# A test-time-training layer with a gated feed-forward on one core: weight pieces issued from another queue, reads of the first tile's scan put first, the last tile's output by batch

## The reference, cut to what matters

```
k = rope(x @ Wk.T);  v = x @ Wv.T                # x: (2, 4096, 512), 16 heads of 32
for each block of 16 tokens (a scan):             # state W: 32x32 per batch and head, from eye
    z = k_block @ W
    W = W - k_block.T @ ((z - v_block) * 2 / (16 * 32))
out = layernorm(z of all blocks, gamma, beta) @ Wo.T
x1  = layernorm(x + out)
y   = (silu(x1 @ gate.T * gate_s) * (x1 @ up.T * up_s)) @ down.T * down_s     # 1408 hidden
result = layernorm(x1 + y)
```

## Time and profile before

| | |
|---|---|
| median of 3 runs | 1947.25 us |
| lowest, highest | 1944.1, 1949.56 us |
| profiled execution, its own time | 1950.08 us |
| its span, first to last instruction | 1948.3 us |
| mean granted TensorE clock | 0.981 |
| PE busy | 1855.2 us (95%) |
| DVE, POOL, ACT busy | 1178.1 (60%), 640.9 (33%), 547.9 us (28%) |
| chain that ended last | PE 73%, DVE 14%, DMA 4%, SP's queue 4% |

### The profile page before, as it was taken

One profiled execution on the slowest core, in us unless ns is written; L12 is line 12 of the kernel. 1 busy time (PEld: TensorE's weight loads), 2 busy tenths in 40 slices (PEclk: granted clock), 3 DMA queues, 4 the chain that ended last, 5 costly groups with the idle time before them and its releaser, 6 DMA issues.

```text
span 1948.3 us, 60606 instructions
## 1 busy us (share of the span) xinstructions
PE 1855.2 (95%) x25792; PEld 1478.8 (76%) x25792; DVE 1178.1 (60%) x2608; ACT 547.9 (28%) x1236; POOL 640.9 (33%) x776
## 2 busy tenths in 40 slices
PE   7569999999999999999999999999999999999897
PEld 4347777777777777777777787777778777777776
DVE  3456666656666666666666566566666666666543
ACT  2122223232322223222222232222322222232222
POOL 2113333333333333333333333333333333333333
PEclk9689999999999999999999999999999999999899
DMA  8665454455455445545445554544554544455210
GB/s 265 214 211 154 135 154 141 139 149 164 148 153 154 125 139 166 166 141 158 138 136 146 163 156 143 153 134 131 167 164 141 155 147 133 145 152 156 84 57 23
DMA packets 302497, 287.26 MB, mean 147 GB/s; under 512 B 42769, under 2 KB 252305, under 8 KB 302097
## 3 DMA queue, kind: packets, MB, share of 16 engines
q1 hardware_dynamic: 295952, 265.26, 45.8%
q10 hardware_dynamic: 6272, 18.09, 2.8%
HBM read 152.65 MB, written 139.20 MB: 150 GB/s over the span
## 4 chain that ended last, share of the span: by engine, by line
PE 73%; DVE 14%; DMA 4%; SPq 4%; ACT 2%; issue 2%; ACTq 0%; POOL 0%; DVEq 0%; POOLq 0%
PE gu_acc L778 31%; PE work L759 21%; PE down_acc L790 12%; PE scan_acc L731 4%; DVE x_tok L945 3%; PE scan_acc L748 3%; DVE state L1016 3%; DVE hid L1021 2%; DVE stats L931 2%; SPq L306 2%; DMA z_scr<-v_rows 2%; ACT hid L562 1%; DVE turned L950 1%; DMA landed<-x1T_scr 1%; SPq L350 1%
## 5 line engine op out<-in xcount | busy, mean ns | idle before, releaser
L496 POOL TENSOR_TENSOR hid_lo<-hid,hid_hi 128x256 fp32r<-128x256 f32 x352 | 263.5, 748 | 646.0 <-ACT hid_hi L572 638.2
L778 PE MATMUL gu_acc<-x_hi,gw 128*128 128x256 f32 x1372 | 376.0, 307 | 8.2 <-DVE hid L1021 2.3
L562 ACT ACTIVATE hid<-gu_acc,gate_scale 128x256 f32<-128x256 f32 x343 | 162.6, 474 | 786.0 <-PE gu_acc L778 786.0
L1021 DVE SCALAR_TENSOR_TENSOR hid<-gu_acc,up_scale,hid 128x256 f32<-128x256 f32 x343 | 165.6, 483 | 319.9 <-ACT hid L562 319.7
L778 PE MATMUL gu_acc<-x_lo,gw 128*128 128x256 f32 x1372 | 340.3, 281 | 0.0
L778 PE MATMUL gu_acc<-x_hi,uw 128*128 128x256 f32 x1372 | 339.7, 280 | 0.0
L778 PE MATMUL gu_acc<-x_lo,uw 128*128 128x256 f32 x1372 | 339.1, 280 | 0.0
L1016 DVE SCALAR_TENSOR_TENSOR state<-scan_acc,half_step,state 128x256 f32<-128x256 f32 x512 | 223.4, 478 | 173.5 <-PE scan_acc L748 168.8
L778 PEld LDWEIGHTS gu_acc<-x_hi,gw 128*128 128x128 f32 x1372 | 258.5, 188 | 44.4 <-DVE hid L1021 18.1
L790 PE MATMUL down_acc<-dw,hid_hi 128*128 128x512 f32 x704 | 282.3, 401 | 2.3 <-POOL hid_lo L496 2.2
L790 PE MATMUL down_acc<-dw,hid_lo 128*128 128x512 f32 x704 | 279.1, 397 | 0.0
(11 more groups left out here) (114 smaller groups left out, 2223.7 us busy)
## 6 DMA issues: line engine op xcount, KB each, us to landing
x_fm<-xT SPq DMA_DIRECT2D x64, 256.0 KB, 3.5
k_scr<-k_tok SPq DMA_DIRECT2D x32, 512.0 KB, 6.7
k_rows<-k_scr SPq DMA_DIRECT2D x512, 32.0 KB, 2.0
z_scr<-v_rows SPq DMA_DIRECT2D x32, 512.0 KB, 3.2
z_tok<-z_scr SPq DMA_DIRECT2D x512, 32.0 KB, 1.8
x_tok<-x SPq DMA_DIRECT2D x32, 512.0 KB, 5.8
out<-x_tok SPq DMA_DIRECT2D x32, 512.0 KB, 3.4
v_rows<-v_scr SPq DMA_DIRECT2D x488, 32.0 KB, 2.0
```

The source lines that it names most:

```text
L496: pool.tensor_tensor(hid_lo[m % RING][:], hid[m % 2][:], hid_hi[m % RING][:].bitcast(F32), ALU.subtract).then_inc(hid_lo_ready, 1)
L562: act.activation(hid[m % 2][:], gu_bank(n, m)[:, 0:TOK], ACT.Silu, scale=gate_scale[:, m:m + 1]).then_inc(silu_done, 1)
L778: mm = pe.matmul(gu_bank(n, m)[:, k * TOK:(k + 1) * TOK], lhsT=w[:, c, m * P:(m + 1) * P].bitcast(dt), rhs=part[:, c].bitcast(dt), start=( ...
L1021: dve.scalar_tensor_tensor(hid[m % 2][:], gu_bank(n, m)[:, TOK:2 * TOK], up_scale[:, m:m + 1], hid[m % 2][:], ALU.mult, ALU.mult).then_inc ...
```

## The change

Four things change.

1. All 24 DMAs of the feed-forward's weights move from ACT's program to POOL's, and to other slots: the four gate copies to tick -1 (ahead of any other wait on POOL), two up copies to tick 0, the rest to tick 1, the last two loads to slot 0 of tick 2. `WEIGHED` puts all twelve looks into tick 2.
2. SP's order in tick 1: z of tile 0 is stored and read first; the store of v(1, 1) comes after the first half of the z reads, and the k rows of tile 1 after all of them. Its v rows are now issued there, by SP, and no longer by ACT.
3. In every tick DVE does the end of tile t-4 (`normalize(2, yn, ...)`) in slot 1, behind `step_state` and the first norm of tile t-2, and not in slot 0.
4. The last tile's output is done by batch and on DVE (`finish_last`), with a pow for each batch on POOL and two stores.

```diff
-WEIGHED = {(1, 13): (0,), (1, 15): (1,), (2, 1): (2,), (2, 3): (3,), (2, 6): (4,), (2, 8): (5,), (2, 10): (6,), (2, 11): (7,),
-           (2, 12): (8,), (2, 13): (9, 10, 11)}
+WEIGHED = {(2, 1): (0,), (2, 2): (1,), (2, 3): (2,), (2, 4): (3,), (2, 8): (4,), (2, 9): (5,), (2, 10): (6,), (2, 11): (7,),
+           (2, 12): (8, 9), (2, 13): (10, 11)}
@@ SP @@
                 if within(t):
                     store_k(t)
+                if within(t) and t != 1:
                     store_v(t, 1)
...
                 if within(sc):
                     load_z(sc, 0, NS // 2, 16)
+                if t == 1:
+                    store_v(t, 1)
...
-                if within(t) and t >= 1:
+                if within(t) and t >= 2:
                     load_k_half0(t)
...
                     load_z(sc, NS - 1, NS, 48)
                 if t == 1:
+                    load_k_half0(t)
+                    load_v_half0(t, 0)
+                    load_v_half0(t, 1)
+                if t == 1:
                     load_x_fm(t + 2)
...
@@ POOL @@
+                    if y == LAST and s == 15:
+                        for b in range(BATCH):
+                            pool.wait_ge(var_done[2], LAST + b + 1)
+                            pool.tensor_tensor(rstd[:, 2, b:b + 1], var_eps[:, 2, b:b + 1], neg_half[:, b:b + 1], ALU.pow
+                                               ).then_inc(rstd_done[2], 1)
...
+                    if t == -1 and s == 11:
+                        for c in range(NC):
+                            copy_ffn(0, c)
+                    if t == 0 and s == 10:
+                        copy_ffn(1, 0)
+                        copy_ffn(1, 1)
+                    if t == 1 and s == 0:
+                        load_ffn(0, 0)
+                        copy_ffn(1, 2)
...
+                    if t == 1 and s == 15:
+                        load_ffn(2, 0)
+                        load_ffn(2, 1)
+                    if t == 2 and s == 0:
+                        load_ffn(2, 2)
+                        load_ffn(2, 3)
@@ ACT @@
-                        for c in range(NC):
-                            copy_ffn(0, c)
...
-                    if t == 1 and s % 4 == 0:
-                        copy_ffn(1, s // 4)
-                    if t == 1 and s % 4 == 2:
-                        load_ffn(0, s // 4)
-                    if t == 1 and s == 12:
-                        load_v_rows(1, 0)
-                    if t == 2 and s in (0, 2, 4, 6):
-                        copy_ffn(2, s // 2)
...
@@ PE, in down() @@
+                    if n == LAST and m == NM - 1 and b == 0:
+                        mm.then_inc(down_done, 1)
@@ DVE @@
+            def finish_last():
+
+                dve.wait_ge(out_stored, 16 * LAST)
+                for b in range(BATCH):
+                    dve.wait_ge(down_done, NM * LAST + NM + b)
+                    dve.tensor_tensor(y_tok[:, b, :], down_acc[b][:], down_scale[:], ALU.mult).then_inc(y_scaled, 1)
+                    dve.wait_ge(y_scaled, 2 * LAST + b + 1)
+                    dve.tensor_tensor(y_tok[:, b, :], y_tok[:, b, :], x1_tok[LAST % 2][:, b, :], ALU.add
+                                      ).then_inc(y_added, 1)
+                    dve.wait_ge(y_added, 2 * LAST + b + 1)
+                    stats_of(2, b, y_tok)
...
+                for b in range(BATCH):
+                    dve.wait_ge(rstd_done[2], LAST + b + 1)
+                    dve.tensor_scalar(y_tok[:, b, :], y_tok[:, b, :], moments[:, 2, b, 0:1], rstd[:, 2, b:b + 1],
+                                      ALU.subtract, ALU.mult).then_inc(y_ready, 1)
...
-                    if within(yn) and s == 0:
-                        normalize(2, yn, 0, y_tok, y_tok, y_ready)
-                        normalize(2, yn, 1, y_tok, y_tok, y_ready)
                     if within(o) and s == (1 if o != LAST else 4):
                         normalize(0, o, 0, z_tok, z_tok, zn_ready)
                         normalize(0, o, 1, z_tok, z_tok, zn_ready)
+                    if within(yn) and yn != LAST and s == 1:
+                        normalize(2, yn, 0, y_tok, y_tok, y_ready)
+                        normalize(2, yn, 1, y_tok, y_tok, y_ready)
```

More of the change, by code:

```diff
@@ L419, in tick @@
                     store_v(t, 0)
-                if within(y):
+                if y == LAST:
+                    for b in range(BATCH):
+                        sp.wait_ge(y_ready, 2 * y + b + 1)
+                        sp.dma_start(out[b, rows(y), :], y_tok[:, b, :]).then_inc(out_stored, 16)
+                elif within(y):
                     sp.wait_ge(y_ready, 2 * y + 2)
@@ L530, in tick @@
                         add_rotated(t + 1, 0)
-                    if within(y) and s == 14:
+                    if within(y) and y != LAST and s == 14:
                         add_residual(y, 0)
                         add_residual(y, 1)
-                    if within(y) and s == 15:
+                    if within(y) and y != LAST and s == 15:
                         inverse_root(2, y)
+                    if y == LAST and s == 15:
[3 more added lines that the diff above has]
+                                               ).then_inc(rstd_done[2], 1)
                     if t == 2 and s == 13:
@@ L540, in tick @@
                                                   bass.bass_isa.ReduceOp.max).then_inc(low_half_known, 1)
+                    if t == -1 and s == 11:
[7 more added lines that the diff above has]
+                        copy_ffn(1, 2)
+                    if t == 1 and s == 2:
+                        load_ffn(0, 1)
+                        copy_ffn(1, 3)
+                    if t == 1 and s == 4:
+                        load_ffn(0, 2)
+                        copy_ffn(2, 0)
+                    if t == 1 and s == 6:
+                        load_ffn(0, 3)
+                        copy_ffn(2, 1)
+                    if t == 1 and s == 8:
+                        load_ffn(1, 0)
+                        copy_ffn(2, 2)
+                    if t == 1 and s == 10:
+                        load_ffn(1, 1)
+                        copy_ffn(2, 3)
+                    if t == 1 and s == 12:
+                        load_ffn(1, 2)
+                    if t == 1 and s == 14:
+                        load_ffn(1, 3)
+                    if t == 1 and s == 15:
[4 more added lines that the diff above has]
+                        load_ffn(2, 3)
             run(tick)
@@ L629, in copy_kT @@
                                ).then_inc(kT_in, 8)
[L631 to L645, removed]
             act.wait_ge(wk_in, 16 * NC)
@@ L1031, in scale_y @@
                     dve.tensor_tensor(y_tok[:, b, :], down_acc[b][:], down_scale[:], ALU.mult).then_inc(y_scaled, 1)
+            def finish_last():
[8 more added lines that the diff above has]
+                    stats_of(2, b, y_tok)
+                    dve.wait_ge(stats_done[2], 2 * LAST + b + 1)
+                    dve.memset(spare[:], 0.0)
+                    dve.bn_aggr(moments[:, 2, b, :], stats[:, 2, b, :]).then_inc(moments_done[2], 1)
+                    dve.wait_ge(moments_done[2], 2 * LAST + b + 1)
+                    dve.tensor_scalar(var_eps[:, 2, b:b + 1], moments[:, 2, b, 1:2], LN_EPS, None, ALU.add
+                                      ).then_inc(var_done[2], 1)
+                for b in range(BATCH):
+                    dve.wait_ge(rstd_done[2], LAST + b + 1)
+                    dve.tensor_scalar(y_tok[:, b, :], y_tok[:, b, :], moments[:, 2, b, 0:1], rstd[:, 2, b:b + 1],
+                                      ALU.subtract, ALU.mult).then_inc(y_ready, 1)
             def low_zn(n, b):
@@ L1097, in tick @@
                         low_x1(o, 1)
-                    if within(yd) and s == (13 if t != WITHOUT_SCAN else 11):
+                    if within(yd) and yd != LAST and s == (13 if t != WITHOUT_SCAN else 11):
                         scale_y(yd)
-                    if within(yd) and s == 15:
+                    if yd == LAST and s == 13:
+                        finish_last()
+                    if within(yd) and yd != LAST and s == 15:
                         dve.wait_ge(y_added, 2 * yd + 2)
```

19 lines of the change are left out of this document (14 added, 5 removed).

## The result

The changed kernel is slower: 1966.44 us median of 4 runs (1960.95 to 1969.83), against 1948.4 us for the kernel before beside it; ratio 1.0091, 95% interval 1.0076 to 1.0105. The forecast was 1946.2 us with a range to 1957, so the direction and the range were both wrong. By the prediction's own signs ("a rotation after 22 is case C") the profile is its case C, the side it gave 25%, and the time is 9.5 us beyond that case's 1956.9. The profiled execution of the changed kernel is the shortest of the four, 1960.95 us (span 1959.1): its trace explains 10.8 us more span than before. The other runs took 5 to 9 us more than it, and have no trace.

A forecast was written before the change was run, and what follows sets the result against it. PE bounds the middle, SP's z stores and reads the start, then DVE's queue. Terms -5.7 - 0.9 - 1.0 + 3.1 + 2.5 + 1.0 = -1.0 us, so a median of 1946.2 us, range 1937 to 1957.

The forecast's parts named there:

- a rotation after 22: Sign in the start: DVE's first rotation, 15.51 us before, coming after 22 us would show case C.
- case C: Start: copies hold wv in whole (+8.1), z stores beside the weights cost +6.0; sum +9.6, 1956.9 us; chance 25%.
- The gate copies in tick -1: Start: POOL's four early copies hold part of wv's load and delay the first rotation; +2.5, between 0 and +8.1.
- The z chain: Ticks 1 and 2: z stored earlier, but rows at the chain's end and weights' traffic; +1.0, between -7.2 and +7.0.
- the looks: Tick 2 on DVE: one look ahead of the state (+1.5), one more from slot 8 on (+1.6); +3.1, bounds 0 and +3.2.
- the bound of +8.1: Start: all four gate copies get ahead of wv, 9.3 us of hold less 1.2 us of room.
- The bound of +7.0: Tick 2: with z stores of 11.4, 8 and 5.5 us, rows land at 91.7 and L731 starts at 95.8.
- The issue on POOL: Ticks -1 to 1: POOL mostly waits, so issuing the weights' DMAs there was taken to cost 0.
- The swap: Middle ticks: DVE's state update 0.9 us earlier removes PE's 28 waits of 0.2 us; -5.7, bounds 0 and -5.7.
- the last tick: Scan's last tick: the state update comes 0.9 us earlier into PE's wait of 3.19 us; -0.9, between 0 and -3.2.
- the end: Behind the last product: last tile by batch on DVE, last store issued at 1944.1, not 1945.09; -1.0, bounds -0.5 and -1.5.
- the forecast's -7.6: Middle and end together: -5.7 for the swap, -0.9 for the last tick, -1.0 for the end.

The follow-up runs named there:

- e1: The kernel before with changes 3 and 4 alone (DVE's last norm, the last tile by batch): 1936.81 us, ratio 0.9947 to the kernel before.
- e4: The changed kernel, but POOL issues the four gate copies only when wv has landed: 1955.13 us, ratio 1.0035.
- e9: The changed kernel, but POOL issues the gate copies when wk has landed, behind all of wv's issues: 1951.67 us, ratio 1.0028.
- e12: The changed kernel with tick 1's k rows moved behind the second z store and v rows behind the third: 1957.22 us, ratio 1.0049.
- e5: e4 with the down pieces copied and loaded by POOL in tick 2, not beside the z chain: 1949.25 us, ratio 1.0011.
- e7: e1 with the changed kernel's WEIGHED (all twelve looks in tick 2), nothing else: 1940.57 us, ratio 0.9967.
- e3: e1 plus change 1 (weights issued early by POOL, looks in tick 2), SP's order and ACT's v rows as before: 1957.86 us, ratio 1.0045.
- e15: The changed kernel with gate copies behind wv, down pieces in tick 2, looks as before, k and v rows between z stores: 1934.87 us, ratio 0.9940.
- e10: e2 with tick 1's k rows moved behind the second z store and v rows behind the third: 1934.01 us, ratio 0.9940.
- e2: e1 plus change 2 (SP's new order, v rows by SP), weights and looks as before: 1937.38 us, ratio 0.9946.
- e8: e2 with the weights' DMAs issued by POOL at the times ACT had: 1933.84 us, ratio 0.9944.
- e13: e10 with SP issuing the load of x for tile 0 first in tick 2: 1931.95 us, ratio 0.9906.
- e14: e11 with SP issuing the load of x for tile 0 first in tick 2: 1931.88 us, ratio 0.9915.
- e11: e10 with looks 4, 5, 6 in slots 4 and 6 of tick 2 and ACT's pieces closer together: 1934.68 us, ratio 0.9936.

## Why the prediction was wrong

**The step that failed** is the weights' traffic, in both of its terms: "The gate copies in tick -1", taken at +2.5, and "The z chain", taken at +1.0. Together with the looks the start was put at +6.6; it lost 21.0 in the profiled execution, and by the medians more (the changed kernel stands 0.0144 above e1, 28 us). By the profile 8.9 us of the 21.0 are there when z's saving begins (2.5 forecast), 9.9 come in the z chain (1.0 forecast) and 2.2 behind it, by the looks (3.1 forecast). The single steps add up to the loss by the medians: gate copies 0.0056 to 0.0063 (e4, e9), rows at the end of the chain 0.0042 (e12), down pieces in tick 1 0.0024 (e5), looks 0.0020 (e7), together 0.0142 to 0.0149. The intervals of each are 0.0011 to 0.0021 either way, and the runs of the changed kernel beyond the profiled one are unseen, so the split between them is rough. The traces split it otherwise: at the feed-forward's first operand e4 gives back 4.7 us, e9 10.1, e12 3.2, and e5 against e4 10.6.

**The gate copies.** The mechanism and its place were named, the middle of the bounds was the wrong choice. The argument was that wv "is issued just before". That holds for one of its four DMAs, issued 0.46 us ahead of the first copy (5.0 us); the other three, issued at 4.64 us and later, took 12.8 to 13.5, and wv is ready only with the last of them. So the cost is the whole hold, not one and a half copies of it: 8.0 us at wv, 6.7 at the rotation, where the bound of +8.1 stood. The rule that the prediction weighed, from the Trainium skill, "DMA: Bandwidth & Descriptors", "Queues, rings and completion order" (turns between queues, a packet at a time), agrees with the packets counted above, 104 and 113 from 9 to 16 us. What it was taken to promise, a wait for only as many packets as wv has, is no relief here, since equal packets aren't equal bytes: in those 7 us the copies moved 2.48 MB and SP's queue 0.22, where the three waiting DMAs are 0.79 MB.

And the delay of 6.7 us didn't end at the rotation: the saving of z began 8.9 us late (45.53 for 36.67), because the two early up copies met ACT's v rows. ACT's reads of v rows took 11.0 us (33.95 to 44.9) and not 8.0; they took 10.7 to 11.9 in e3, e4, e9, e12 and e15, which have the early up copies too, and 8.8 in e1. That collision stood in no term. It isn't always on the path: e15 has it and is as fast as e10.

**The z chain.** The bound of +7.0 was built of stores as dear as the trace had (11.4 and 5.5 us are in rows 10; for the second, priced at 8, the row has 3.61). That is no ceiling for a change that adds traffic to the same place: the first store took 14.6 us, the second 2.8, the third 8.2. Nor was the first issued at 48.6 us, as forecast, but at 59.19; the order alone brought it to 50.61 (e2). Taking 8.9 us of earlier delay off, PE's second step was 9.9 late by itself. e5 is the test of the cause: the same store took 10.1 us with the down pieces gone. The order was judged rightly: "z is ready earlier, but DVE can't use it before the rows are there"; that this is free without traffic (e2) and costs 8 us with it (e12) follows from that sentence, but the forecast had no case that put both together at this size. Case C had the mechanism and the sign (25%), with 14.1 us for what cost some 19 in the profiled execution and 24 by the medians.

**The looks.** +3.1 forecast, +2.2 in the profiled execution behind PE's second step, 4 by e7 (not clear of noise). PE's wait in slot 2 went from 1.78 to 3.43 us, as said.

**The issue on POOL**, taken at 0: right (e8). Its issues took 0.49 to 0.84 us. The other rule that was weighed, of the Trainium skill's "SBUF — State Buffer", "SBUF: two separate sides" (descriptors of POOL's DMAs starve beside certain modes of DVE), isn't seen in e8's time; no run here was made to show it.

**The swap, the last tick, the end.** -5.7 forecast; -7.1 in the changed kernel's trace, -9.5 in e1's. The wait of the row went whole, as said; the other 1.4 to 3.8 us aren't explained, and lie within the 7 us by which this stretch differs between kernels whose ticks are alike. The last ticks gave 1.4 (forecast 0.9), with the clock at 1.00 from 1800 to 1830 us where it had been 0.83. The last store's issue came 0.9 nearer to the last product (forecast 1.0), and since it now holds half as much the span ended 0.8 sooner behind it (2.4 us and not 3.2). e1's interval, -6 to -14 us, holds the forecast's -7.6.

## What to carry to other kernels

A bulk DMA that is freed to start early holds whatever is still queued when its packets begin: order it behind the last issue of the transfer that the start hangs on (2.6 us later at the issue gave 12 us back), and keep it out of the stretches where a chain of store and read sets the pace. A bound on such a cost taken from the dearest row before is a bound only if the traffic beside it stays the same. When a chain gets shorter and the time doesn't follow, look at what is issued behind an unrelated wait on the same queue: one load, moved ahead of it, gave 0.0034 (e13; 0.0021 in e14 against e11) where both reorderings of the chain gave 0.0007, though the first is barely clear of noise and the others aren't. The version with the lowest ratio (e13, 1931.95 us, 0.9906) keeps the weights on ACT at their old times.

## What the runs showed of the hardware

- Four DRAM-to-DRAM copies of 704 KB, issued from 4.62 us on, did no harm to a 256 KB load issued 0.46 us ahead of them (5.0 us to landing) and held the next three, issued at 4.64 us and later (12.8 to 13.5). With the copies issued 2.6 us later the four landed after 4.6 to 5.5 us. SP's small loads behind them took 11 to 12 us to land (3.6 to 4.6 before), and the issue of one of 64 KB held SP for 4.71 us (0.43 before).
- From 9 to 16 us in that trace the copies' queue and SP's moved 104 and 113 packets, but 2.48 and 0.22 MB: about equal turns by packet, with data packets of 44 KB and 2 KB.
- With the DMA engines' share at 0.97 to 0.99 in all three, a 512 KB store took 14.6 us beside 3.90 MB of weights, 10.1 beside 2.19 (e5) and 9.0 beside 2.12 (e1).
- A plain DMA issued by POOL took 0.49 to 0.84 us of it, and a kernel with all 24 weight DMAs on POOL at the same times ran as fast as with them on ACT.
